# Two-layer conditioned attention block on one core: the first x set in earlier, the weights' stages set in by arrival, idle multiplications on TensorE taken out

## What is computed

```
m = silu(cond) @ w_ada + b_ada            # nine shifts, scales and gates per batch
# layer 0
h = ln(x)*(1+sc_msa)+sh_msa;  q,k,v = roll(h @ w_qkv + b_qkv, -64)
x += g_msa * (roll(window_attention(q,k,v), 64) @ w_so + b_so)      # windows of 128, 16 heads of 16
h = ln(x)*(1+sc_mca)+sh_mca;  q = h @ w_q;  k,v = ctx @ w_kv
s = q k^T / 4;  keep the 16 largest of 256 in each row;  softmax;  x += g_mca * ((p @ v) @ w_co + b_co)
h = ln(x)*(1+sc_mlp)+sh_mlp;  a,b = h @ w_m1;  x += g_mlp * ((silu(a)*b) @ w_m2 + b_m2)
# layer 1
q from ada_ln(x), k,v from ada_ln(ctx), full attention, x += (p @ v) @ Wp + bp
```

## Time and profile before

| | |
|---|---|
| median of three runs | 1345.95 us |
| profiled execution, as timed | 1343.52 us |
| its span | 1341.7 us |
| mean granted clock of TensorE | 0.977 |
| TensorE busy | 1233.3 us, 92% |
| VectorE busy | 1146.4 us, 85% |
| ScalarE busy | 994.8 us, 74% |
| GpSimd busy | 875.2 us, 65% |

### The profile page before, as it was taken

How to read it: one execution, slowest core, us unless ns; L and a number is a source line. 1 busy time by engine, 2 the same in 40 slices (tenths; PEclk the granted TensorE clock), 3 DMA queues, 4 the chain that set the end, 5 groups by cost and what they waited for, 6 DMA issues and landing times. The chain is left out here.

```text
span 1341.7 us, 39506 instructions
## 1 busy us (share of the span) xinstructions
PE 1233.3 (92%) x14013; PEld 874.8 (65%) x14013; DVE 1146.4 (85%) x3819; ACT 994.8 (74%) x2001; POOL 875.2 (65%) x1161
## 2 busy tenths in 40 slices
PE   6678789989999999999999999999999999989887
PEld 6566466656666676767676766666666756656654
DVE  4418999989999999999999999999999999896322
ACT  3343577869888787979797979888787968776743
POOL 0132468867868586869586876868685857666630
PEclk9888999989999999999999999999999999999998
DMA  6420202121213031212122121213020211110010
GB/s 209 140 55 20 64 22 53 37 61 26 73 26 80 9 80 29 66 32 61 45 53 53 33 66 26 65 38 82 16 73 14 59 47 42 26 31 20 25 33 17
DMA packets 111392, 67.28 MB, mean 50 GB/s; under 512 B 13836, under 2 KB 107870, under 8 KB 111198
## 3 DMA queue, kind: packets, MB, share of 16 engines
q1 hardware_dynamic: 111198, 64.76, 17.9%
...
## 5 line engine op out<-in xcount | busy, mean ns | idle before, releaser
L1248 ACT ACTIVATE prob<-turned_score 128x1024 f32<-128x1024 f32 x320 | 326.4, 1020 | 108.7 <-PE turned_score L947 102.9
L1478 POOL TENSOR_TENSOR pair<-full,pair 128x512 f16<-128x512 f32 x192 | 221.0, 1160 | 140.7 <-ACT pair L1222 137.2
L1484 POOL TENSOR_SCALAR far<-far 128x512 bf16<-128x512 bf16 x256 | 158.0, 617 | 77.2 <-DVE far L1413 57.7
L1386 DVE TENSOR_REDUCE rowmax_l<-score 128x4 f32<-128x1024 f32 x128 | 156.0, 1219 | 61.2 <-PE score L947 50.3
L1399 DVE MATCH_REPLACE8 rest<-top,score 128x256 f32<-128x256 f32 x512 | 208.2, 415 | 0.0
L1413 DVE MATCH_REPLACE8 far<-best,rest 128x256 bf16<-128x256 f32 x512 | 205.5, 409 | 0.0
L1396 DVE MAX8 top<-score 128x8 f32<-128x256 f32 x512 | 192.7, 418 | 4.9 <-PE score L947 4.8
L947 PE MATMUL work<-pair_n,w_m_hi 128*128 128x256 f16 x1024 | 172.8, 273 | 1.5 <-issue 1.4
L947 PE MATMUL work<-pair_n,w_m_lo 128*128 128x256 f16 x512 | 139.6, 273 | 0.0
L1463 POOL TENSOR_SCALAR rstd_n<-mean_var_n 128x2 f32<-128x2 f32 x64 | 12.6, 197 | 190.2 <-DVE mean_var_n L1378 187.2
L1222 ACT ACTIVATE pair<-full 128x512 f16<-128x512 f32 x192 | 121.0, 630 | 19.0 <-DMA q_stack_l<-pair 1.0
...
## 6 DMA issues: line engine op xcount, KB each, us to landing
...
```

The source lines that it names most:

```text
L1248: act.activation(prob[:, at:at + 2, :], both_b[:, :, :], ACT.Exp).then_inc(exp_done, 1)
L1386: dve.tensor_reduce(rowmax[s][n % 2][:, :].rearrange("p (z m) -> p z m", z=2)[:, :, at:at + wide], both_a[:, :, :].rearrange("p z (h k) -> ...
L1478: pool.tensor_tensor(pr[:, 1, :, :], whole[:, :, :], pr[:, 0, :, :], ALU.subtract).then_inc(split_lo, 1)
L1484: pool.tensor_scalar(tile, tile, FAR, -1.0, ALU.add, ALU.mult).then_inc(far_fixed, 1)
```

## The change

Three things change in the text, and no arithmetic of the result.

1. The idle multiplications and the waits ahead of them are gone.
2. The numbers in WEIGHTS lie closer to those of the batches:

```diff
 WEIGHTS = (
-    ("sp", "wd:0@-820.48184 wd:1@-815.84396 wd:2@-760.47169 wd:3@-638.08125 wd:4@-637.89492 wd:5@-572.64794 "
...
-            "wd:12@-392.89263 wd:13@-361.08397 wd:14@-349.29088 wd:15@-341.82081 wd:16@-334.33457 "
-            "wd:17@-214.76897 wd:18@-178.65186 wd:19@-104.2353 wd:20@-38.57571 wd:21@-35.09744"),
...
+    ("sp", "wd:0@-604.08253 wd:1@-584.93518 wd:2@-437.64361 wd:3@-419.23981 wd:4@-410.78658 wd:5@-386.45165 "
+            "wd:6@-365.25013 wd:7@-232.92814 wd:8@-199.26512 wd:9@-174.55477 wd:10@-90.75979 wd:11@-90.68389 "
+            "wd:12@-85.52493 wd:13@-1.99414 wd:14@3.64956 wd:15@4.51892 wd:16@27.83298 wd:17@35.40098 "
+            "wd:18@54.57426 wd:19@66.01109 wd:20@72.81765 wd:21@99.54617"),
...
 SHIFTS = {
...
-    0: "xi:0@-218.3515 bn_n1:0@-110.89574 rs_n1:0@-80.70304 x4_n1:0@-239.39815 sp_n1:0@-143.58704 "
+    0: "xi:0@-245.63865 bn_n1:0@-205.08334 rs_n1:0@-163.49411 x4_n1:0@-292.28138 sp_n1:0@-224.03255 "
...
-IDLE_WORK = ("wp:0:14=119 x4_n1:0:0=24 pj_wq:0:0=45 wp:0:19=21 a_w:0:2=21 bk_w:0:0=18 pr_w:0:0=7 xt_w:0:0=17 "
-             "x4_n2:0:0=24 pj_tq:0:0=45 a_w:1:0=30 a_w:1:2=21 a_t:0:0=31 a_w:1:3=20 bk_w:1:0=25 pr_w:1:0=43 "
-             "a_t:0:4=10 a_t:0:7=25 a_t:1:0=7 bk_t:15:0=10 x4_n4:14:0=15 xt_t:15:0=17 a_l:14:3=15 bk_l:13:0=8 "
-             "xt_m:15:0=17 x4_n4:15:0=34 pj_lq:15:0=17 a_l:15:0=26 bk_l:14:0=8 a_l:15:3=9 a_l:15:7=14 "
-             "o_l:15:3=17 bk_l:15:0=18 pr_l:15:0=43")
...
             for piece, b, i in plan["pe"]:
                 kind, _, s = piece.partition("_")
-                if (piece, b, i) in idle:
-                    if o_begun > 0:
-                        pe.wait_ge(osum_done, o_begun)
-                    for _ in range(idle[piece, b, i]):
-                        mm(bank_c[:, L:L + P], ident16[:, :], ident16[:, :], True, True)
```

More of the change, by code:

```diff
@@ L46 @@
 WINDOW = (
[L47 to L58, removed]
+    ("sp", "xi:0@-170.0394 in_wq:0@-33.93172 in_wk:0@-21.80413 gg_w:0@-6.59753 gg_w:1@-0.93554 gg_w:2@7.54226 "
+            "gg_w:3@8.40826"),
@@ new lines @@
+    ("pe", "x4_n1:0@-7.20142 pj_wq:0@-2.69253 pj_wk:0@4.45101 vj_w:0@6.72634 a_w:0@26.99925 a_w:1@29.35941 "
+            "gd_w:0@31.92404 a_w:2@31.99303 gd_w:1@32.40069 gd_w:2@34.52004 a_w:3@38.8861 b_w:0@38.98702 "
+            "o_w:0@41.243 gd_w:3@41.28037 b_w:1@42.54466 b_w:2@45.29654 o_w:1@46.10591 o_w:2@48.49512 "
+            "b_w:3@49.15154 o_w:3@52.41891 ot_w:0@53.54497 bk_w:0@56.64833 pr_w:0@60.65559 xt_w:0@62.45433"),
+    ("act", "sp_n1:0@-5.53475 sp_wq:0@1.42537 sp_wk:0@5.17352 v_w:0@8.08995 gc_w:0@32.22542 gc_w:1@32.70852 "
+            "gc_w:2@37.79167 e_w:0@40.59588 os_w:0@43.83445 gc_w:3@44.18078 e_w:1@44.54591 e_w:2@46.58753 "
+            "os_w:1@48.11303 e_w:3@52.03468 os_w:2@52.65622 os_w:3@54.16928 sp_ws:0@58.15491 fo_w:0@62.31335"),
@@ L59 @@
+    ("dve", "bn_n1:0@-18.19193 rm_w:0@23.9695 rm_w:1@27.81271 rm_w:2@29.03094 rm_w:3@40.13031 nv_w:0@54.71258 "
+            "xa_w:0@62.08375"),
+    ("pool", "rs_n1:0@-21.72809 lo_n1:0@-8.47042 lo_wq:0@2.65784 lo_wk:0@9.51467 lo_ws:0@54.77226"),
 )
 TOP = (
[L62 to L68, removed]
@@ L78 @@
[L78 to L81 removed]
+    ("sp", "ct:0@-83.5314 in_tk:0@-38.75452 in_tq:0@-24.37698 gg_t:0@2.66555 gg_t:1@21.19081 gg_t:2@35.5703 "
+            "gg_t:3@44.62465"),
@@ new lines @@
+    ("pe", "pj_tk:0@-8.31842 x4_n2:0@1.6462 pj_tq:0@10.72122 a_t:0@25.19689 a_t:1@37.19846 a_t:2@40.41142 "
+            "gd_t:0@41.45438 b_t:0@46.42601 a_t:3@48.65576 b_t:1@48.90973 vj_t:0@49.4606 gd_t:1@52.45279 "
+            "a_t:4@53.19063 b_t:2@59.86464 a_t:5@61.02066 o_t:0@62.50238 a_t:6@66.25962 b_t:3@67.5818 "
+            "gd_t:2@68.10656 o_t:1@76.21073 b_t:4@80.10924 a_t:7@80.24042 gd_t:3@82.9167 b_t:5@83.53282 "
+            "o_t:2@86.39466 b_t:6@86.72766 b_t:7@89.68654 o_t:3@94.071"),
@@ L110 @@
-    ("pool", "rs_nc:0@-31.91531 lo_nc:0@-7.68812 rs_n4:0@6.7945 lo_n4:0@9.64603 lo_lk:0@18.65644 lo_lq:0@21.99394 "
-            "lo_ls:0@122.565"),
+    ("sp", "cl:0@-124.28479 in_lk:0@-15.81556 in_lq:0@-10.04222 gg_l:0@7.33241 gg_l:1@25.11324 gg_l:2@35.27825 "
+            "gg_l:3@49.29648 xo:0@105.38461"),
+    ("pe", "x4_nc:0@-17.87362 x4_n4:0@14.31642 pj_lk:0@18.60819 pj_lq:0@21.27087 a_l:0@36.18544 a_l:1@41.23124 "
+            "vj_l:0@42.49455 gd_l:0@42.65817 a_l:2@49.16519 a_l:3@50.27952 b_l:0@50.33488 a_l:4@52.17505 "
+            "b_l:1@52.86886 a_l:5@53.98419 gd_l:1@54.36136 o_l:0@58.29889 gd_l:2@64.86543 b_l:2@68.31123 "
+            "a_l:6@68.48951 b_l:3@72.90403 a_l:7@74.18313 o_l:1@76.1949 b_l:4@79.392 b_l:5@84.41364 "
+            "gd_l:3@87.65848 o_l:2@90.909 b_l:6@98.12233 b_l:7@105.09309 o_l:3@107.64772 ot_l:0@116.67945 "
+            "bk_l:0@118.98012 pr_l:0@125.45662"),
@@ L112 @@
+    ("pool", "rs_nc:0@-31.63044 lo_nc:0@-17.64307 rs_n4:0@4.44942 lo_n4:0@8.65571 lo_lk:0@15.10704 "
+            "lo_lq:0@20.99104 lo_ls:0@122.08356"),
 )
 WEIGHTS = (
[L115 to L118 removed]
```

777 lines of the change are left out of this document (380 added, 397 removed).

## The result

The changed kernel takes 1331.97 us (median of 1331.14, 1328.44 and 1332.79; one further execution, of 3440.6 us, was disturbed and is left out), the kernel before 1346.88 us on the same chip. The medians differ by 14.9 us. The ratio is 0.9881 with a 95% interval of 0.9855 to 0.9906, which is 16 us (13 to 20) less, where 10.5 had been forecast. The profiled execution has a span of 1329.3 us and 1331.14 as timed. Against the profiled span of before, 1341.7, it is 12.4 us shorter, and those 12.4 us are what two traces can be asked about.

What follows compares the result with a forecast made beforehand. TensorE and VectorE, both full at 72 us per middle batch, bound the kernel, so an earlier first top-8 passes to the end. −15.9 + 3.9 + 0 + 1.5 = −10.5 us gave 1335.5 us, range 1326 to 1347.

Steps and rivals of the forecast that it cites:

- the 15.9 forecast: Head: VectorE's first top-8 was to start at 89.4 us instead of 105.33, 15.9 us earlier.
- The first x and the first score: Head: x issued behind five weight transfers lands at 14.2 us; first score at 37.6, 18.4 us earlier.
- From the first score to the first top-8: Head: 49.4 us before, minus 3.1 for idle blocks, plus 4 for the clock, plus 1.5 for the order.
- SP's queue: Head: the query input waits behind a weight transfer held by batch 1's row maximum, allowing the first top-8 at 89.
- the data's own path: Head: without the queue limit, the clock, order and idle-block terms put the first top-8 at 89.4 us.
- Removing the idle multiplications: Head and tail: 3.1 us gained in the head, 4 lost there to the clock, 1.5 lost at the end.
- Behind the first top-8: +3.9: After the first top-8: later batch 1 exponentials make VectorE wait, +3.1, +1.6 and −0.8, together 3.9 us lost.
- the clock is what the idle work bought: Rival, chance 0.09: head and tail run slow throughout without idle work; 1345.7 us, no change.
- The middle: 0: Middle batches: the same stages with some places changed, 72 us per batch, no gain or loss.
- The repeated pattern: Batches 3 to 9: a transposing stage set back leaves its top-8 reader 1.2 us of cover out of 2.9.
- the rival of the swaps: Rival, chance 0.11: swapped places cost time in the full middle, up to thirteen times; slower, 1352 us at 1.3 per batch.
- The tail: +1.5: End of the kernel: 1 us gained from removed idle work, more lost to the clock; net 1.5, between −1.5 and +8.

Runs made afterwards that it cites:

- e8: The kernel before with only the first x's transfer moved ahead of the sixth weight transfer on SP's queue; ratio to before 1.0003.
- e3: The changed kernel with the first x issued right behind the first weight transfer instead of behind the fifth; ratio to before 0.9846.
- c2: The same kernel as e3, run again on another chip as the measure for edits beside it; ratio to before 0.9844.
- e2: The kernel before without its idle multiplications, nothing else changed; 1356.1 us, ratio to before 1.0052.
- e4: The changed kernel with batch 0's top-8 query input ahead of weight transfer wd:20 on SP, and that weight's splits set later; ratio to before 0.9890.
- e9: e3 with batch 0's top-8 query input ahead of weight transfer wd:20 on SP and that weight's splits set slightly later; ratio to before 0.9851.
- e1: The changed kernel with the 34 blocks of idle multiplications put back, two at a neighbouring stage; 1341.6 us, ratio to before 0.9939.
- e6: The changed kernel with batch 1's turned score ahead of batch 0's top-8 value projection on TensorE; ratio to before 0.9884.
- e7: The kernel before with x of batch 6 moved ahead of batch 4's query weights' input on SP's queue; ratio to before 0.9994.

## Why the prediction was right, and where it was wrong

**The direction, the bound and the size.** Right: the forecast was 1335.5 us within 1326 to 1347, the measured median 1331.97. What the change moves on VectorE at the start arrives at the end, less what is given back behind it. The head was most of the gain, 11.8 of 12.4 us in the two traces. That the total came out so near is in part luck. The head fell 4.1 us short of the 15.9 forecast, and the gains in batch 2 and batches 10 to 14, 7.5 us together, which the forecast had at nothing, made up for it.

**The first x and the first score.** Forecast 14.2 and 37.6, measured 14.72 and 39.03. From the statistics to the first score 24.3 us against 23.4: `wp:4` and the slow projections were priced about right, 0.9 short. The experiments split the credit: the transfer by itself is worth 0 (e8), and issuing x behind five weights instead of one left 3 to 5 us lying at the first statistics and the first MAX8 (e3, c2).

**From the first score to the first top-8.** Forecast 51.8 us, measured 54.5. The sum added 4 for the clock and 1.5 for the order and took off 3.1 for the idle blocks. Up to the first row maximum of batch 1 clock and order cost 4.1 together: the way from the first row maximum to the end of the addition to x took 30.4 us against 27.4, at a granted clock of 0.59 against 0.77, and from there 15.1 against 14.1. That is less than the 5.5 forecast. The two steps that failed lie behind it. `wp:19` between the first two scores of batch 1 had no term, though the orders show it: at the low clock it takes 3.59 us, and the second row maximum follows the first by 4.07 us instead of 1.99, so it costs 2.1. And taking out the idle blocks gave 1.0, not 3.1: from the second row maximum to the first MAX8 it takes 4.16 us against 5.19, because the score then waits for row maxima as well as for the copies. e2 shows the same in the old order: from the first row maximum of batch 1 to the first MAX8 6.3 us without the blocks, 7.2 with them.

SP's queue was seen rightly as the second path, with the right row maximum at its head: it was forecast 0.4 us from the data's own path and came within 0.15 of it (e4, e9). Its times were early by 4 us: k's copies of batch 1 were to be issued from 74 to 78 and were issued from 77.57 to 82.12, and the row maximum ended at 86.5, not 81.8. Of that 1.4 us was the later first score and 2.4 the way from it to those copies, 38.5 us where I had 36.1.

**Removing the idle multiplications.** The terms were small, −3.1 in the head, +4 for the clock, +1.5 at the end. The net of that in the new order is wrong in sign and size: with the blocks kept the changed kernel is 8 to 10 us slower (e1). The error was to cost the blocks where the old order had them. The order and the blocks are one change: removing them costs 7 us in the old order and brings 8 to 10 in the new one. The rival "the clock is what the idle work bought" fits the sign in the old order and is wrong for the new.

The Trainium skill, page "TensorE: Matmul & The Clock Gate", Part 1, The HAM clock gate, says that the throttled state is the default and that activity releases it. e1's granted clock agrees with it (0.77 against 0.60 from 39 to 90 us). What the prediction drew from that for the time does not hold in the new order: in the same run the first MAX8 came 9.1 us later, with 6.81 us of padding on the way to it.

**Behind the first top-8: +3.9.** The sum came out, +4.3 us in batch 0, and the mechanism did not. The stall was to grow at nv_w:1's RECIPROCAL from 1.74 to some 5.6 us; it is 1.91. The first exponential of batch 1 did start 3.1 us later than before, 4.9 us behind the first MAX8 (98.47) instead of 1.9; it waited for the turned score of batch 1, and `wh:21` would have held it to within 0.7 us of there (e6). But of the 4.7 us that I let it and sp_n1:2 cost, 1.7 were left when the last of the four sums was evicted (16.7 us behind the first MAX8 against 15.0), and x4_n1:2 leaving ot_w:1's way gave back 1.65, not 0.8. So nothing was left for RECIPROCAL. The 4.3 us are 2.2 more at waits of the MAX8 for scores (2.8 against 0.6), 1.3 at the addition to x, 0.2 at RECIPROCAL, and 0.7 for the split `wl:21`, which now lies behind the first top-8 instead of ahead of it, less 0.3 at row maxima. I took the low clock for the cause of the first two. In e1, at a higher clock, the MAX8 waits 1.3 us and the addition 1.7, so the clock may have a part in the first and doesn't explain the second. Their cause is open.

**The middle: 0.** The repeated pattern cost nothing, 0.2 us over seven batches, so the rival of the swaps fell and the 1.2 us of cover for t1:6 were enough. But it was not 0: −4.3 in batch 2 and −3.2 in batches 10 to 14. I had looked for waits that the swaps might add and not for those that were there and might go; the 3.31 us in front of a row maximum stood in the trace of before. e7 shows x's part in it at that row maximum and in that period (2 to 3 us), not in the sum of the batches and not in the time.

**The tail: +1.5.** +0.9 in the first pair of traces. The nine traces of the new order have 182.4 to 185.6 us, and the three of the old order with the blocks 180.8 to 181.9, so the true figure is nearer to 2 or 3. The terms were not measured one by one; the bound of plus 8 for the clock was far too wide.
